# Twelve extra constant products in the first group's solve of a grouped-whitening kernel

## The reference

```
x: (32, 128, 56, 56) f32, weight, bias: (128, 1)
y   = group_norm(x, 32 groups of 4 channels, eps 1e-5)
cov = y_g y_g^T / M + 1e-4 I           16 groups of 8 channels, M = 32*56*56, y centred per channel
x  + (cov^-1/2 y_g) * weight + bias
```

## Time and profile before

| | us |
|---|---|
| median of 3 runs | 392.31 (391.88 to 394.16) |
| profiled execution | 394.99 |
| its span, first to last instruction | 393.1 |
| TensorE matmul busy | 333.5 (85%) |
| VectorE busy | 308.2 (78%) |
| ScalarE busy | 303.9 (77%) |
| GpSimd busy | 288.1 (73%) |
| mean of the records' granted TensorE clock | 0.994 |

### The profile page before, as it was taken

The page is one execution under the profiler, slowest core; times in us unless marked ns, Lnnn a source line. Parts: engine busy times, 40 slices in busy tenths (PEclk is TensorE's granted clock), DMA queues, the critical chain, the costliest instruction groups (busy, mean ns, idle before and its releaser), DMA issues.

```text
span 393.1 us, 8416 instructions
## 1 busy us (share of the span) xinstructions
PE 333.5 (85%) x3140; PEld 206.9 (53%) x3140; DVE 308.2 (78%) x854; ACT 303.9 (77%) x449; POOL 288.1 (73%) x148
## 2 busy tenths in 40 slices
PE   0114366999999999999999999999999999998891
PEld 0113354665656665656565656565656566554450
DVE  2679999879999999999999999999999984531100
ACT  1056576669899999999999999999999898944561
POOL 0049999878989898989898989898989898920000
PEclk9999999999999999999999999999999999999997
DMA  7999999804899999999999998999994545355668
GB/s 221 271 301 308 311 328 311 283 19 148 276 307 310 316 323 325 321 321 312 301 305 298 310 336 286 304 307 324 310 318 144 186 132 179 128 200 170 208 210 282
DMA packets 18888, 103.70 MB, mean 264 GB/s; under 512 B 6432, under 2 KB 6432, under 8 KB 14752
## 3 DMA queue, kind: packets, MB, share of 16 engines
q1 hardware_dynamic: 18848, 103.18, 80.4%
HBM read 51.77 MB, written 51.38 MB: 262 GB/s over the span
## 4 chain that ended last, share of the span: by engine, by line
PE 80%; POOL 9%; SPq 3%; ACT 2%; DVE 2%; DMA 1%; issue 1%; DVEq 0%
PE ps_apply L562 50%; PE ps_small L562 14%; PE ps_gram L562 13%; POOL hl_ring L323 8%; PE ps_stat L562 3%; SPq L279 2%; POOL ring L315 2%; DMA wb<-in_L_conv_bias_dram 1%; ACT hl_ring L517 1%; ACT tz L535 1%; DVE bn L339 1%; DVE pp L424 0%; DVE t_ring L398 0%; ACT ring L526 0%; SPq L291 0%
## 5 line engine op out<-in xcount | busy, mean ns | idle before, releaser
L323 POOL TENSOR_TENSOR hl_ring<-ring,hl_ring 128x1024 f16<-128x1024 f32 (+1 forms) x96 | 230.9, 2417 | 31.5 <-ACT hl_ring L517 31.5
L562 PE MATMUL ps_apply<-ring,a_t 128*128 128x392 f32 x512 | 203.5, 523 | 0.0
L339 DVE BATCH_NORM_STATS2 bn<-ring 128x6 f32<-128x448 f32 x224 | 129.0, 604 | 9.3 <-DMA ring<-in_x_dram 9.3
L517 ACT CAST hl_ring<-ring 128x1024 f16<-128x1024 f32 (+1 forms) x96 | 129.1, 1372 | 4.0 <-DVE t_ring L398 2.8
L526 ACT ACTIVATE ring<-ps_apply,fin_add 128x784 f32<-128x784 f32 x128 | 115.7, 904 | 20.3 <-PE ps_apply L562 20.3
L398 DVE STREAM_TRANSPOSE t_ring<-hl_ring 128x1024 f32<-128x1024 f32 (+1 forms) x96 | 119.3, 1242 | 3.5 <-POOL hl_ring L323 3.2
L562 PEld LDWEIGHTS ps_apply<-ring,a_t 128*128 128x128 f32 x512 | 88.1, 191 | 43.2 <-ACT ring L526 2.3
L562 PE MATMUL ps_gram<-t_ring 128*128 128x64 f16 x1568 | 69.0, 200 | 11.6 <-DVE t_ring L398 11.6
L315 POOL TENSOR_SCALAR ring<-ring,y_mul,y_add 128x1024 f32<-128x1024 f32 (+1 forms) x48 | 58.0, 1214 | 26.3 <-DVE y_add L385 26.0
L505 ACT ACTIVATE ring<-ring,y_add,y_mul 128x1024 f32<-128x1024 f32 (+1 forms) x48 | 60.1, 1252 | 9.4 <-DVE y_add L385 8.1
L562 PEld LDWEIGHTS ps_gram<-t_ring 128*128 128x128 f16 x1568 | 58.7, 102 | 14.8 <-DVE t_ring L398 12.1
(11 more groups left out here) (59 smaller groups left out, 176.4 us busy)
## 6 DMA issues: line engine op xcount, KB each, us to landing
ring<-in_x_dram SPq DMA_DIRECT2D x256, 196.0 KB, 4.1
out_dram<-ring SPq DMA_DIRECT2D x128, 392.0 KB, 4.9
cst<-const_dram SPq DMA_DIRECT2D x1, 380.0 KB
wb<-in_L_conv_weight_dram SPq DMA_DIRECT2D x1, 0.5 KB
wb<-in_L_conv_bias_dram SPq DMA_DIRECT2D x1, 0.5 KB
```

The costliest lines, as they stand in the source:

```text
L323: nc.gpsimd.tensor_tensor(hl[:, :, 0], ring[:, g % RING, s, px], hl[:, :, 1], ALU.subtract).then_inc(l_ready, 1)
L339: nc.vector.bn_stats(bn[:, g % 2, s, c, :], ring[:, g % RING, s, c * BN:(c + 1) * BN]).then_inc(bn_done, 1)
L517: nc.scalar.copy(hl_ring[:, i % HL_RING, 0:width(p), 1], ring[:, g % RING, s, px]).then_inc(h_ready, 1)
L562: return nc.tensor.matmul(out_, lhsT, rhs, start=start, stop=stop, skip_group_check=True)
```

## The change

Behind each of the hops 16, 17 and 18 of group 0, TensorE does four products of two constants (`avg`, 128x128, as weights, and `every`, 128 columns) into the fourth bank of ps_apply. Nobody reads the result, nothing waits for it and it signals nothing; the first apply step that uses this bank overwrites it. The signal of the hop itself stands ahead of its four products.

```
+WARM_HOP, WARM = HOP_T, 4
...
+            def keep_clock(times):
+                for _ in range(times):
+                    product(ps_apply[:, 3, 0:P], k_("avg"), k_("every"))
...
                 if k == HOP_ROOT:
                     ins = product(s_root[e], zx[:, e], res[:, e])
                 ins.then_inc(solve_mm[e], 1)
+                if g == 0 and k >= WARM_HOP:
+                    keep_clock(WARM)
```

## The result

The changed kernel is slower. Its median is 396.34 us (392.82 to 399.36, 20 runs) against 393.56 us (391.58 to 395.82, 20 runs) for the kernel before; the ratio is 1.0059, 95% interval 1.0036 to 1.0081. The ratios leave out executions over 1.5% above the fastest of their kernel, here four of the changed kernel's (from 398.8 us), further down one in e1, two in e8 and four in e10; the ratio of the two medians is 1.0071. The forecast was 391.1 us and a range up to 395.2, so the sign and the size are both wrong: against its own kernel before the changed one was to be 1.2 us faster, and it is 2.8 us slower. The profiled execution took 395.63 us with a span of 393.8 us.

What follows compares the result with a forecast made beforehand. TensorE bounds the kernel from about 69 us. Hop 2 late +2.9, earlier clock -4.6, stall +0.5 sum to -1.2 us: 394.99 becomes 393.8, less 2.7 for the median gives 391.1 us; range 389.9 to 395.2 us.

Steps and rivals of the forecast that it cites:

- Bound and frame: Whole kernel: from about 69 us, time added to or taken from TensorE's queue reaches the end, if other engines follow.
- Cost of the lots: TensorE behind hops 16 to 18: three lots of four products take about 5.5 us, making hop 2 3.8 us late at most.
- The 0.15 us of the forecast: Start of each lot on TensorE: the first weight load, not hidden behind a tiny product, adds some 0.15 us.
- Gain and stall: TensorE from 69.13 to 80.87 us: earlier clock rise gives back 4.6 us, waits for other engines lose 0.5 us.
- The 0.2 us for a_t: Behind late hop 2: VectorE has a_t ready at about 74.9 us, TensorE would be there about 0.2 us before.
- ScalarE's turnaround between hops 3 and 4: Group 1's hops: TensorE at the upper clock loses 0.3 us to it, covered by a long Gram piece at the lower.
- ScalarE's and VectorE's other late reads: Behind the late hops: ScalarE's read waits some 2 us, but is covered; uncovered it would cost up to 2 us.
- where the clock rises: TensorE's lots: rise near the start of the third lot, about 70.3 to 71 us; forecast chance 0.5.
- the forecast's bound: TensorE behind HOP_T: the same 8.06 us of work would put the clock's rise at 74.1 us at the latest.
- The transfer to the median: Whole kernel: the median's 2.7 us below the profiled run was carried over, turning 393.8 into 391.1 us.
- the clock of the usual run already rises earlier: Rival on the kernel before: the median run's clock rises sooner than the profile's, so no gain, 392.4 to 393.2 us; chance 0.2.
- The slower rival: TensorE's queue, 66 to 72.9 us: products slow it and the clock rises no sooner, 394.2 to 396.1 us; chance 0.27.

Runs made afterwards that it cites:

- e1: The changed kernel again without edit, for a second profile; median 396.58 us, ratio 1.0067 against the kernel before.
- e8: Kernel before plus products in early TensorE waits, four behind hop 0 of group 0, two behind hops 1 to 15, one behind 16 to 18; 395.31 us, ratio 1.0038.
- e10: Kernel before plus products filling TensorE's waits from 23 us to the first apply step, two behind each further hop of group 0; 397.25 us, ratio 1.0014.
- e4: Kernel before plus 12 products in TensorE's waits 18 to 28 us ahead of HOP_T, none behind the last hops; 394.35 us, ratio 1.0004.
- e13: The changed kernel without edit, profiled again to look for the place of the clock's rise; 393.97 us.
- e14: The changed kernel without edit, one more profile to look for the place of the clock's rise; 395.86 us.
- e5: The kernel before, unchanged, for a second profile; 394.51 us.
- e11: Kernel before plus products filling TensorE's waits from 23 us to the first apply step, one behind each further hop of group 0; 396.66 us, ratio 1.0077.
- e3: Changed kernel with all 12 products in one stretch behind HOP_ROOT of group 0; 395.67 us, ratio 1.0051 against the kernel before.
- e2: Changed kernel with the same 128x128 weights but only 2 columns streamed per product; 396.72 us, ratio 1.0076 against the kernel before.

## Why the prediction was wrong

**Bound and frame: right.** TensorE is the bound from 69 us on, and a delay at the third apply step reaches the end whole (the rest is 312.2 to 313.0 us everywhere). The low clock until 80.9 us, read from durations against the column, was right too (e4).

**Cost of the lots: mis-sized by 0.5 us.** A record takes 0.21 us as forecast, but a lot takes 2.00 us from its start to the next hop's, not 1.72 + 0.15, since its first weight load shows whole: it takes 0.29 us, and eight records at 0.214 us follow (0.29 + 8 x 0.214 = 2.00). The 0.15 us of the forecast stood on no row; the earlier trace rows, with 0.58 us for the first record against 0.21 for the next, already had room for the larger term. 6.0 us instead of 5.5; hop 2 came 4.3 us late with the clock down, where I took 3.8, and 3.14 with the rise ahead of the third lot (e13), where I took 2.9.

**Gain and stall: right in size, the stall by luck.** In e13 hop 2 to the third apply step took 14.23 - 6.40 = 7.83 us. Before it was 15.00 - 3.26 = 11.74 us, so 3.9 us came back: 4.6 forecast less 0.5 of stall is 4.1. The stall that was measured is 0.23 + 0.35 = 0.58 us: a transpose, and VectorE's read of hop 4, which hop 5 waits for. The forecast's two terms were others. The 0.2 us for a_t didn't come (a_t is ready at 74.92 us, TensorE asks for it at 75.24), and the wait for ScalarE's turnaround between hops 3 and 4 is 0.26 us in e13 and in the kernel before alike. That ScalarE's and VectorE's other late reads would be covered was right.

**The step that failed: where the clock rises.** I took the likeliest case from one analogy, 8.06 us of apply and Gram work for 7 us of lots, and gave 0.5 to a rise inside or right behind the lots. In six profiles it rose inside the lots once (at the end of the second), behind hop 3 twice, in the first apply step twice and at its end once. Within the forecast's bound, 74.1 us or 8.2 us behind HOP_T, lies only e13 (4.7 us); e14 and e1 rose 8.9 and 9.3 us behind HOP_T, between hops 3 and 4, the others 13.2 to 13.9 us behind it. By the medians the lots paid back 4.3 - 2.8 = 1.5 us of the 4.3 that they cost.

**The transfer to the median: the second failure.** Of the 5.2 us between 391.1 and 396.34, 1.25 us are the base (the median of three executions was 392.31 us, that of twenty is 393.56) and 4.0 us the change (+2.8 instead of -1.2). I carried the 2.7 us between the profiled run and the median over as if both had the same clock history. The rival *the clock of the usual run already rises earlier* fits the times: 13.1 us seems to be as much the kernel before's case as 15.0 (e4; e5's spread of times), though no profile of that kernel shows it. The median of 393.56 us answers to 13.7 us (393.56 - 1.9 - 312.4 - 65.6, the mean start of HOP_T). By this reckoning even the lucky case e13, with 14.23 us, wins nothing. I priced this rival at 392.4 to 393.2 us for a rise inside the lots; with the five later rises, 15.4 to 17.0 us, it gives 395.3 to 396.9.

**The slower rival** came nearest: 394.2 to 396.1 us was its range, the median is 396.34. Of its 0.27 I left the upper half outside the range. Its mechanism holds in part. The queue pays in full, and the rise mostly comes too late to pay it back; but the clock did rise sooner behind HOP_T in all six profiles (4.7 to 13.9 us) than in the two of the kernel before (15.1 and 15.4 us). Whether it does so against the faster executions of the kernel before, which no profile shows, is open: in e4, without products near it, the last rise came 10.4 us behind HOP_T.

The Trainium skill (TensorE: Matmul & The Clock Gate, "What's actually happening") says that the activity is looked at in windows that run free of the kernel. The six profiles of one kernel, with the rise at four different places of the work, agree with this; I cited it and gave it no weight in the sum.

**What stays open.** Why the clock rises in one execution of a kernel here and in the next there: no profile shows what decides it. The fastest executions of the changed kernel (392.8 us) were not caught in a profile; e13 with 393.97 is the nearest. How dense the work between a rise and the first apply step must be for the clock to stay up was not measured.

## What to carry to other kernels

Products that only keep the clock up are paid at the low rate, at the one point of the queue where they stand; put ahead of the stretch where TensorE becomes the bound, they made the queue 4.3 us late in five of six profiles (3.1 in the sixth). Against the 15.00 us of the kernel before, the third apply step was then 1.7 to 2.0 us late where the clock rose in or at the end of the first apply step, 0.4 us late where it rose behind hop 3, and 0.8 us early only where it rose inside the lots. A few products in long waits, away from the chain, cost nothing measurable and won nothing (e4). Behind every hop of the dependent chain they fit only while the clock is up: if it falls, they take twice the time and become the chain (e11). When a trace's clock history can differ between executions, look at several profiles of the kernel before, and at the spread of its times, before a sum is made against one of them.

## What the runs showed of the hardware

- The views of the granted clock read 1.00 from the start of a kernel until the first change (no kept trace has a clock entry ahead of its first rise), while the durations are those of 1.2 GHz; after a fall it reads 0.50 for the same durations (e4: 1.03 us for a Gram piece of 16 either way).
- The clock can fall again within about 3.5 us of a rise, without an idle time longer than 0.34 us: in e3 between the Gram piece at 75.54 us (fast) and the apply step at 76.75 us (slow).
- The place of the rise differs between executions of one program: 14.2 to 17.0 us from HOP_T to the third apply step in six profiles, and a spread of 7 us in 30 timed runs, against 5 us (391.0 to 395.8) in 102 timed executions of the kernel before.
- One more execution of the kernel before took 485.2 us at a mean granted clock of 0.709, against 0.992 to 0.995 in the 82 others whose mean is on record. No profile caught it, and its cause is open.
- Products of 128x128 f32 weights cost nearly the same with 2 columns as with 128 (1.80 against 2.00 us for four at the lower clock); the eight weight loads of a lot take 1.78 us in both (e2 and the changed kernel). None of the ten executions with the narrow ones was faster than 395.86 us.
